# Head 0's row maxima between the units of the query and key projection, with the projection's quarters in another order

## The reference

```python
x = x + _layernorm(_L0_attn_ref(_layernorm(x), W_qkv, W_proj))
# _L0_attn_ref, 16 heads of 32 columns
qkv = x @ W_qkv.T
q, k, v = jnp.split(qkv, 3, axis=-1)
attn = jnp.einsum('bhqd,bhkd->bhqk', q, k) * SCALE
attn = jnp.where(causal[None, None], attn, -jnp.inf)
probs = jax.nn.softmax(attn, axis=-1)
out = jnp.einsum('bhqk,bhkd->bhqd', probs, v)
```

## Time and profile before

| what | us |
|---|---|
| median of three executions | 1799.64 |
| lowest and highest | 1797.62, 1800.24 |
| the profiled execution, its own time | 1802.54 |
| span of the profiled execution, first to last instruction | 1800.8 |
| TensorE, matmuls shown busy | 1673.1 (93% of the span) |
| VectorE busy | 1167.4 (65%) |
| ScalarE busy | 1099.9 (61%) |

### The profile page before, as it was taken

The page is one execution under the profiler, slowest core; times in us unless marked ns, Lnnn a source line. Parts: engine busy times, 40 slices in busy tenths (PEclk is TensorE's granted clock), DMA queues, the critical chain, the costliest instruction groups (busy, mean ns, idle before and its releaser), DMA issues.

```text
span 1800.8 us, 31014 instructions
## 1 busy us (share of the span) xinstructions
PE 1673.1 (93%) x9215; PEld 1383.0 (77%) x9215; DVE 1167.4 (65%) x2385; ACT 1099.9 (61%) x1668; POOL 949.9 (53%) x828
## 2 busy tenths in 40 slices
PE   6998899999999999999786799999999999999990
PEld 6976576777767767676565799999999999999980
DVE  5522777777777777778478565665665566566544
ACT  2211278888787877887467465665665565556542
POOL 2310288888878888887554234433433433443324
PEclk9998599999999999999898799999999999999995
DMA  7566211111222111110391688888888887888768
GB/s 231 166 182 184 55 48 48 48 47 47 53 69 66 48 47 47 47 47 25 114 349 32 225 249 238 253 248 238 255 247 236 243 227 218 224 245 231 209 166 196
DMA packets 103221, 276.86 MB, mean 154 GB/s; under 512 B 19851, under 2 KB 37643, under 8 KB 93131
## 3 DMA queue, kind: packets, MB, share of 16 engines
q1 hardware_dynamic: 76059, 212.25, 36.5%
q0 software_dynamic: 27056, 63.31, 17.1%
HBM read 194.76 MB, written 63.72 MB: 144 GB/s over the span
## 4 chain that ended last, share of the span: by engine, by line
PE 41%; DVE 3%; POOL 3%; DMA 2%; issue 2%; ACT 1%; POOLq 0%; DVEq 0%; ACTq 0%
PE p_prj L85 24%; PE p_at_ps L85 6%; PE p_logit_ps L85 6%; PE p_ht_ps L1859 3%; PE p_at_ps L1882 2%; DMA m_gate<-acc_rows 1%; DMA acc_rows<-m_y_out,m_row_ids 1%; POOL rows L1251 1%; POOL p_rstd L1237 1%; DVE r_lane_hot L1564 1%; ACT r_edge_hot L1340 1%; DVE p_st L1576 1%; DVE p_st L1570 1%; DMA gathered<-h_rows,m_row_ids 0%; POOL p_minus L1235 0%
## 5 line engine op out<-in xcount | busy, mean ns | idle before, releaser
L584 POOL TENSOR_TENSOR prob_lo<-prob,prob_hi 128x1024 fp32r<-128x1024 f32 x217 | 465.6, 2166 | 128.1 <-DVE prob_hi L664 125.1
L636 DVE TENSOR_REDUCE part_max<-a_mp 128x1 f32<-128x512 f32 (+3 forms) x640 | 382.8, 610 | 77.6 <-PE a_mp L727 45.2
L1273 POOL DMA_INDIRECT acc_rows<-m_y_out,m_row_ids x109 | 177.6, 1629 | 418.0 <-ACT m_y_out L1444 393.3
L620 ACT ACTIVATE prob<-a_sp 128x1024 f32<-128x1024 f32 x320 | 293.6, 929 | 101.5 <-PE a_sp L790 65.7
L85 PE MATMUL p_prj<-m_w_hi,m_ht_hi 128*128 128x352 f32 x888 | 298.0, 336 | 1.4 <-DVE m_ht_lo L1673 1.4
L85 PE MATMUL p_prj<-m_w_lo,m_ht_hi 128*128 128x352 f32 x888 | 289.1, 326 | 0.0
L85 PE MATMUL p_prj<-m_w_hi,m_ht_lo 128*128 128x352 f32 x888 | 288.4, 325 | 0.0
L1697 DVE TENSOR_TENSOR m_w_lo<-m_w_raw,m_w_hi 128x704 fp32r<-128x704 f32 (+1 forms) x357 | 271.1, 798 | 22.9 <-ACT m_w_hi L1450 22.4
L1450 ACT ACTIVATE m_w_hi<-m_w_raw 128x704 fp32r<-128x704 f32 (+1 forms) x357 | 229.0, 714 | 16.8 <-PE p_prj L85 16.8
L1683 DVE TENSOR_TENSOR m_at_lo<-p_at_ps,m_at_hi 128x384 fp32r<-128x384 f32 x111 | 61.8, 557 | 252.4 <-ACT m_at_hi L1436 252.4
L607 ACT ACTIVATE prob_hi<-prob 128x1024 fp32r<-128x1024 f32 x216 | 203.3, 941 | 6.9
(11 more groups left out here) (232 smaller groups left out, 3331.7 us busy)
## 6 DMA issues: line engine op xcount, KB each, us to landing
m_w_raw<-wexp SPq DMA_DIRECT2D x51, 1408.0 KB
m_w_raw<-wexp SPq DMA_DIRECT2D x51, 768.0 KB
qk_parts<-rows SPq DMA_DIRECT2D x64, 256.0 KB, 3.0
multi<-qk_parts SPq DMA_DIRECT2D x48, 256.0 KB, 4.8
acc_rows<-p_zeros SPq DMA_DIRECT2D x2, 4352.0 KB, 17.4
v_head<-v_all SPq DMA_DIRECT2D x16, 520.0 KB, 3.1
k_stack<-qk_parts SPq DMA_DIRECT2D x24, 256.0 KB, 4.0
q_stack<-qk_parts SPq DMA_DIRECT2D x24, 256.0 KB, 6.2
```

The lines of the kernel that those rows point to most:

```text
L584: nc.gpsimd.tensor_tensor(prob_lo[:, t % RING, :, c0:NB], prob[:, t % RING, :, c0:NB], f32(prob_hi[:, t % RING, :, c0:NB]), ALU.subtract). ...
L620: nc.scalar.activation(prob[:, t % RING, :, c0:NB], sp_[:, t % 2, :, c0:NB], ACT.Exp, scale=SCALE).then_inc(prob_ready, 1)
L636: nc.vector.reduce_max(part_max[:, qb, kb:kb + 1], mp[:, n % 2, 0:width], AX_X).then_inc(piece_done, 1)
L1273: nc.gpsimd.indirect_dma_start(acc_dram[sum_of(t)], bass.IndirectOffsetOnAxis(ap=row_id(t), axis=0), y_out[:, t % 4, :], None, compute_op= ...
```

## The change

Head 0's 40 pieces leave the attention stage. They are placed behind units 19 to 29 of the projection, three behind units 19, 21, 24 and 27, and four behind each of the others. For that the quarters now run K, Q, K, Q (`QK_ORDER`), so that after 16 units head 0's K and Q are both parked; Q is loaded ahead of the park of unit 16 instead of 24. Pieces go through the PSUM tile `vp` (free after V), their maxima into `xn`, the turned maxima through `tp`. Part a is turned behind unit 26 and sent behind the park of unit 27, part b behind units 30 and 31. Units 16 to 31 are written out on every engine instead of looped. The stage of attention starts with the scores of tile 0, which wait for both parts of the maxima (`head0_max_landed`).

The core of the diff; counts of semaphores that shift by one head, and the removal of `first_pieces`, are left out:

```diff
+QK_ORDER = (2, 0, 3, 1)
+HEAD0_FROM = 19
+HEAD0_UNITS = 11
+def head0_pieces(n):
+    i = n - HEAD0_FROM
+    if not 0 <= i < HEAD0_UNITS:
+        return range(0)
+    return range(i * NPC // HEAD0_UNITS, (i + 1) * NPC // HEAD0_UNITS)
...
-                    if base == 0:
-                        for n in range(NTB):
-                            unit(n, n % 2, q, f, n)
+                    if base == 0 or base >= QK_PIECES // 2 * PIECE_UNITS:
+                        for tb in range(NTB):
+                            unit(base + tb, tb % 2, q, f, tb)
...
-                for at, stack, parts in ((PIECE_UNITS, 0, (2, 3, 2)), (3 * PIECE_UNITS, 1, (0, 0, 1))):
+                for at, stack, parts in ((PIECE_UNITS, 0, (2, 3, 2)), (2 * PIECE_UNITS, 1, (0, 0, 1))):
...
+            nc.gpsimd.memset(f32(multi[ROW_MAX:ROW_MAX + 1, 0, :]), 1.0).then_inc(head0_ones, 1)
...
                 dve.wait_ge(unit_hi_done, n + 1)
                 nc.vector.tensor_tensor(qk_lo[:, k, :], qp[:, k, :], f32(qk_hi[:, k, :]),
                                         ALU.subtract).then_inc(unit_lo_done, 1)
+                for part in head0_turned_at(n):
+                    maxima_out(part)
+                for i in head0_pieces(n):
+                    piece(i)
...
+            def piece(i):
+                qb, kb, k0, k1 = piece_keys(i)
+                if i == 0:
+                    pe.wait_ge(head0_landed, 16 * KQ_LOADS)
+                    pe.wait_ge(v_lo_done, NT)
+                    pe.wait_ge(masks_step, MASK_STEPS)
+                if i >= 2:
+                    pe.wait_ge(piece_done, i - 1)
+                diagonal = k1 == (qb + 1) * P
+                last = nc.tensor.matmul(vp[:, i % 2, 0:k1 - k0], multi[0:K_ROWS, 1, qb * P:(qb + 1) * P],
+                                        multi[0:K_ROWS, 0, k0:k1], start=True, stop=not diagonal)
...
-            sp.wait_ge(max_a_out, 1)
-            send_max_a(0)
+            sp.wait_ge(head0_max_landed, 32)
...
-            pe.wait_ge(kq_landed[0], 16 * KQ_LOADS)
-            for n in range(NPC_A):
-                piece(0, 0, n)
-            turn_maxima(0, "a")
...
                     if t == 0:
                         if first:
-                            pe.wait_ge(ones_set, 2)
-                        pe.wait_ge(max_a_landed[p], visit * 16 + 16)
+                            pe.wait_ge(head0_max_landed, 32)
+                        else:
+                            pe.wait_ge(max_a_landed[p], (visit + p) * 16)
```

More of the change, by code:

```diff
@@ L86, in three_passes, with piece_keys, head0_ready, head0_turned_at @@
     return last
+PIECES = [(qb, kb) for qb in range(NT) for kb in range(qb // 4 + 1)]
+NPC = len(PIECES)
+QA = 12
+NPC_A = sum(1 for qb, _ in PIECES if qb < QA)
+K_ROWS, ROW_MAX = 3 * HD, 3 * HD
+KQ_LOADS = 6
+QK_ORDER = (2, 0, 3, 1)
+MASK_STEPS = 7
+HEAD0_FROM = 19
[5 more added lines that the diff above has]
+    return range(i * NPC // HEAD0_UNITS, (i + 1) * NPC // HEAD0_UNITS)
+def piece_keys(n):
+    qb, kb = PIECES[n]
+    return qb, kb, kb * NB, min((kb + 1) * NB, (qb + 1) * P)
+def head0_ready(part):
+    return (NPC_A if part == "a" else NPC) - 1
+def head0_turned_at(n):
+    return [part for part in "ab" if head0_ready(part) in head0_pieces(n - 1)]
 def attention_constants(nc, pool, step, ident, ident_r, mask_q, mask_k, mask_f):
@@ L108, in attention_constants, with stage_embed_qkv @@
     make(nc.gpsimd.tensor_copy(mask_k[:], mask_f[:]))
-def stage_embed_qkv(nc, x_dram, wqkv_dram, rows, v_all, ident, ln_consts, qk_dram, multi, head0_landed, parked, masks):
+def stage_embed_qkv(nc, x_dram, wqkv_dram, rows, v_all, ident, ln_consts, qk_dram, multi, head0_landed, head0_max_landed, parked, masks):
     with ExitStack() as ctx:
@@ L196, in park @@
             def park(n, k, q, f, tb):
[L197 removed]
+                which, row = QK_ORDER[q] // 2, (QK_ORDER[q] % 2) * PIECE + f * P
                 sp.wait_ge(unit_lo_done, n + 1)
@@ L259, in _ @@
             attention_constants(nc, pool, masks_step, ident, mask_f=xn[:, 0, 0:2 * P], **masks)
+            for slot in range(2):
+                pool.wait_ge(xT_copied[slot], 32 * NT // 2)
+            nc.gpsimd.memset(f32(multi[ROW_MAX:ROW_MAX + 1, 0, :]), 1.0).then_inc(head0_ones, 1)
         @block.scalar
@@ L384, in unit, with piece, turn_maxima @@
                                         xT_hi[:, c, toks], xT_lo[:, c, toks]), KC).then_inc(unit_ready, 1)
+                if not isinstance(n, int):
+                    return
+                for part in head0_turned_at(n):
+                    turn_maxima(part)
+                for i in head0_pieces(n):
+                    piece(i)
+            def piece(i):
+                qb, kb, k0, k1 = piece_keys(i)
+                if i == 0:
[7 more added lines that the diff above has]
+                                        multi[0:K_ROWS, 0, k0:k1], start=True, stop=not diagonal)
+                if diagonal:
+                    last = nc.tensor.matmul(vp[:, i % 2, k1 - k0 - P:k1 - k0], masks["ident_r"][:], masks["mask_q"][:],
+                                            start=False, stop=True)
+                last.then_inc(piece_ready, 1)
+            def turn_maxima(part):
+                lo, hi = (0, QA) if part == "a" else (QA, NT)
+                pe.wait_ge(row_max_done, 1 if part == "a" else 2)
+                if part == "a":
+                    pe.wait_ge(xt_lo_done, NT)
+                else:
+                    pe.wait_ge(max_out, 1)
+                nc.tensor.transpose(tp[0:hi - lo, 0, 0, :], row_max[:, lo:hi], ident[:]).then_inc(max_turned, 1)
             qk_units(pe, unit)
@@ L394 @@
 RING = 5
-PIECES = [(qb, kb) for qb in range(NT) for kb in range(qb // 4 + 1)]
-NPC = len(PIECES)
-QA = 12
-NPC_A = sum(1 for qb, _ in PIECES if qb < QA)
 PIECES_AT = (0, 0, 0, 0, 0, 3, 4, 3, 4, 2, 1, 2, 1, 3, 3, 3, 3, 3, 3, 2)
@@ L442, in count_before, with stage_attention @@
     return sum(1 for s in which if s < t)
-def stage_attention(nc, rows, v_all, ident, qk_dram, multi, head0_landed, parked, masks, flat, wproj_dram, wgate_dram,
+def stage_attention(nc, rows, v_all, ident, qk_dram, multi, head0_landed, head0_max_landed, parked, masks, flat, wproj_dram, wgate_dram,
                     wproj_landed, spent):
@@ L672, in low_part @@
                                         f32(prob_hi[:, t % RING, :, c0:NB]), ALU.subtract).then_inc(lo_dve, 1)
-            for n in range(NPC_A):
-                piece(0, n)
-            row_maxima(0, "a")
-            maxima_out(0, "a")
             def head(h, p, visit, first, last):
                 for t, (j, kp, c0) in enumerate(S_TILES):
-                    if first:
-                        for n in first_pieces(t):
-                            piece(0, n)
-                    if t == (FIRST_AT[-1] + 1 if first else 0):
+                    if t == 0 and not first:
                         row_maxima(h, "b")
@@ L704, in head @@
                     what = SHARED_AT.get(t)
-                    if what == "max_b":
+                    if what == "max_b" and not first:
                         maxima_out(h, "b")
@@ L806, in head @@
                         pe.wait_ge(v_landed[p], visit * 16 + 16)
-                    if first:
-                        for n in first_pieces(t):
-                            piece(0, 0, n)
+                    if first and t == NS - 1:
+                        pe.wait_ge(ones_set, 1)
                     if t == 0:
                         if first:
-                            pe.wait_ge(ones_set, 2)
-                        pe.wait_ge(max_a_landed[p], visit * 16 + 16)
+                            pe.wait_ge(head0_max_landed, 32)
+                        else:
+                            pe.wait_ge(max_a_landed[p], (visit + p) * 16)
                     scores(h, p, t)
```

91 lines of the change are left out of this document (55 added, 36 removed).

## The result

Four executions of the changed kernel took 1810.27 to 1815.94 us, median 1813.59. The kernel before, beside them, had a median of 1799.87. The ratio is 1.0078, with a 95% interval of 1.006 to 1.0095: the change makes the kernel 13.7 us slower. The forecast was slower by 9 us, 1808.6, in a range of 1801 to 1816. The profiled execution of after took 1813.48 us and its span is 1811.7.

What follows compares the result with a forecast made beforehand. It took head 0's 39.0 us stretch at the low clock, with pieces ahead of and among its tiles, as the cost attacked. Terms 31 + 4 + 0 - 27 + 1 = +9 gave 1808.6 us, range 1801 to 1816.

Steps and rivals of the forecast that it cites:

- Part 1: Projection units 19 to 29: third and fourth pieces wait for VectorE's reductions behind the unit's end, +31 us.
- Part 2: Projection units with pieces: TensorE's idle gaps bring two falls of the clock at 2 us each, +4 us.
- rival 1: No fall of the clock among the units with pieces: +5 us, 1804.6 us; chance 0.17.
- Part 3: Projection: Q's loads at unit 16 instead of 24, other quarter order, units written out; the stall only moves, 0 us.
- Part 4: Attention's start: head 0 without its 40 pieces takes 13.4 us to head 1's first piece instead of 40.5, -27 us.
- Part 5: Behind head 0's entry: TensorE comes cold into tile 5, 2 to 4 us at half speed, +1 us.
- Rival 2: The clock stays low in most units with pieces: eight falls instead of two, 1820 us; chance 0.09.
- Rival 3: No difference: head 0's entry at -30, shorter waits and no fall, 1799.6 to 1802 us; chance 0.14.
- Rival 4: Faster: pieces run beside the units, gap before the third piece below 0.3 us, -16 us, 1784 us; chance 0.10.

Runs made afterwards that it cites:

- the gap filled: The changed kernel with five unused matmuls behind the second piece of each of units 19 to 29; 1800.50 us, ratio 1.0022 to the kernel before.
- the order alone: The kernel before with quarters K, Q, K, Q, Q's load at unit 16, units 16 to 31 written out, pieces left in attention; 1794.42 us, ratio 0.9986.
- Four buffers: The changed kernel with a second PSUM tile, so four buffers for the pieces instead of two; 1783.12 us, ratio 0.9921 to the kernel before.
- the reductions first: The changed kernel with a unit's first two reductions ahead of its low part on VectorE; 1791.63 us, ratio 0.9971 to the kernel before.
- The ten units: The changed kernel with four PSUM buffers and all pieces behind units 19 to 28, four each; 1780.89 us, ratio 0.9906 to the kernel before.

## Why the prediction was right, and where it was off

**Part 1, the chain: right.** Forecast +31, from a third piece 2.16 us behind the unit; the trace shows 2.17. The fourth waited less than reckoned, 0.16 us instead of 0.35. For ten of the eleven units the forecast's terms give 31.7 less one unit of 2.5, so 29.2; the kernel with the gap filled measures 30.0 at the full clock. For all eleven, from the high part of unit 15 to that of unit 31, it takes 78.75 us against 46.69 with the order alone: 32.1 more. The last matmul of unit 31 came 33.75 us later, against 31 and 4 for the clock. Four buffers and the reductions first show that this is the buffer's wait and not the work: the same pieces cost 9.6 without it.

**Part 2, the clock: right in kind, low in number.** Forecast two falls at 2 us, so 4. Over the ten units there were three, which cost 61.40 - 56.68 = 4.7, so 1.6 each. A fourth low stretch lies at unit 20, whose period is 7.37 in the changed kernel and 4.94 in the one with the gap filled. That is 2.4 more, so 7.1 in all, and it stands behind a gap of 4.60 us, which unit 19's third piece had because the parks of the stall held its unit's high part. I had let the stall move eight units forward and had not asked what the first unit with pieces would do behind it. By the medians the filled gap is worth some 10 us. From the high part of unit 15 to that of unit 31 its trace is 7.3 and 6.9 us shorter than the two traces of the changed kernel. The rest comes up in the stage of the experts, where both programs are the same, and is not explained.

The Trainium skill (TensorE: Matmul & The Clock Gate, "Why this matters for your kernels") puts throughput drops in mid-kernel down to idle gaps between bursts that are longer than any among units 21 to 24 here. Here the trace disagrees. From 151.3 to 171.6 us the clock was 1.00 with gaps of 1.27, 1.48, 1.16 and 1.55 us behind the second pieces of units 21 to 24 and none longer, and at 171.65, just behind the last of them, the matmuls of TensorE's timeline go from 0.40 to 0.63:

```profile
170.79 0.44 PE L483 MATMUL e_vp<-multi 96*128 96x384 f32 x1 [1.55 <-DVE xn L411]
171.07 0.22 PE L486 MATMUL e_vp<-mask_q,ident_r 128*128 128x128 f32 x1
171.13 0.45 PE L85 MATMUL e_qp<-xT_hi,e_w_hi 128*128 128x512 f32 x1
171.41 0.40 PE L85 MATMUL e_qp<-xT_lo,e_w_hi 128*128 128x512 f32 x1
171.65 0.50 PE L85 MATMUL e_qp<-xT_hi,e_w_lo 128*128 128x512 f32 x1
171.94 0.63 PE L85 MATMUL e_qp<-xT_hi,e_w_hi 128*128 128x512 f32 x1
```

Filling those gaps took the falls away. So rival 1, whose time the rule gave too, falls. Another section of that page, "A second HAM failure mode: psum-queue depth-cycling", tells of a kernel whose clock swings because of frequent short idles while it cycles through PSUM buffers. By that section falls could be expected here, and the trace agrees; I had not weighed it.

**Part 3, the loads and the order: nearly right.** Forecast 0. The stall behind the load at unit 16 held unit 18's high part for 6.54 us, as the earlier trace rows had it at unit 26 (6.81), and no piece waited for head 0's loads. Written out it costs 0, all three together gain 2.7 us, which I had not seen. I had moved the stall "with its cold restart", and both traces with the early load and no pieces show no such restart. That this is the whole of the gain stays open.

**Part 4, head 0's entry: right.** Forecast -27, from 13.4 us in the place of 40.5; measured -27.05. The first scores waited for the last maxima as forecast, in TensorE's timeline of after,

```profile
214.29 0.79 PE L874 MATMUL a_sp<-multi 97*128 97x512 f32 x1 [5.08 <-DMA multi<-xn]
...
224.05 0.31 PE L815 MATMUL a_mp<-k_stack,q_stack 96*128 96x128 f32 x1
```

and head 1's first piece followed without a wait of its own 9.76 us later (forecast 9.4). Its loads fall due close to that point: the last was issued at 216.6, and the slowest of the three took 7.1 us to land, so 223.7 at the latest. The ten units confirm it: there the maxima came sooner, and the wait for the loads appeared at once, 2.81 us.

**Part 5, the clock behind it: right.** Forecast +1; from head 1's first piece to its scores 34.01 against 32.34 us, +1.67, the clock 0.92 in that stretch against 0.98.

**What was mis-sized.** The projection came out at +34.9 between units 15 and 31 against 31 + 4 + 0 = 35, but not by the terms of the sum. By the traces it is 32.1 for the pieces, 7.3 for the clock and, against the trace of before, -4.4 for the loads and the order (-2.1 against the trace of the kernel with the units only written out, and -2.7 by the medians). The clock was put some 3 us too low and the loads and the order some 2 to 4 us too high, and the two errors cancel. That much of the agreement is luck.

The sum at head 1's first scores is +8.4 in the traces, against a forecast of +9. At the end of the span it is +10.9, and by the medians +13.7. I had set the forecast 2.9 us lower than the trace's own sum, because the profiled execution of before lay that much above its median. After's profiled execution lies on its median (1813.48 and 1813.59), so some 2.8 of the 4.7 us by which the measured difference of the medians exceeds +9 are this: with 1802.54 the difference is 10.9. The other 2 us arose behind the attention stage, where nothing changed. The kernel with the units only written out, equal to before in time, has its end of attention at 858.95 us, 5.35 sooner than the trace of before, and 4.4 of that are there already at unit 31. So a single trace is not worth more than that at such a point.

**The rivals.** Rival 2 (clock low in most units) would have had eight falls, and there were four, the one at unit 20 counted. Rival 3 needed an entry of -30 and no fall; the entry was -27. Rival 4 was the right sum for another kernel: its point of decision was a gap before the third piece of under 0.3 us, and it was 1.44. The kernels in which it has gone or nearly gone are the fast ones, 1781 to 1792 us, where the rival said 1784.

## What to carry to other kernels

Extra work is not hidden merely because the engines have idle time in sum. Where instructions stand in one fixed order, ask what the third piece waits for when there are two buffers, and follow that wait back: if it ends in an operation that the engine itself has only just issued, every unit pays the whole round trip (here 2.17 us to the third piece). Then take it away either with two more buffers, or by putting the new work inside the unit and its consumer ahead of the unit's own tail; here the one took 28 us off and the other 25, and a loss of 14 became a gain of 12 or more. And when a stall is moved, ask what the first unit with new work does behind it.

## What the runs showed of the hardware that was not expected

Among gaps of 1.06 to 1.62 us, one in each unit, TensorE's clock fell from 2.4 to 1.2 GHz, though not behind each. The falls came behind gaps of 1.43 to 1.55, and gaps of that size and a longer one (1.62, behind unit 26) passed without one. In two executions there were three low stretches in ten units, each less than 4 us long, at a price of some 1.6 each. Five spare matmuls of 0.23 us per unit kept it at 1.00. A single gap is a weak sign: behind idles of 3.01 and 4.60 us the clock was low, and behind 2.78 and 2.90 (both above) and 3.21, in the kernel with the gap filled, it was not (TensorE's timeline of the latter, with the next unit's matmuls at 0.40):

```profile
136.60 0.44 PE L487 MATMUL e_vp<-multi 96*128 96x384 f32 x1 [3.21 <-DVE xn L412]
...
137.22 0.40 PE L85 MATMUL e_qp<-xT_lo,e_w_hi 128*128 128x512 f32 x1
```
